# Cross attention on one Trainium2 core: the context's two halves made during self-attention and loaded from DRAM for each head

## The reference: what is computed

```
x = layernorm(x + self_attention(x))            # 16 heads of 128, causal
x = layernorm(x + cross_attention(x, ctx, ctx)) # below
x = layernorm(x + ffn(x))                       # ternary weights: signs of W_g, W_u, W_d

# cross_attention(q, k, v, gamma): 8 heads, cut along the rows
qh, kh, vh = (m.reshape(B, 8, 64, 512) for m in (q, k, v))   # k = v = context
qk  = einsum('bhdq,bhdl->bhql', qh, kh) / sqrt(64)
ret = einsum('bhql,bhdl->bhdq', softmax(qk), vh)
return gamma * ret.reshape(B, 512, 512)
```

## Time and profile before

| | us |
|---|---|
| median of three runs | 1504.17 (1502.49 to 1505.21) |
| the profiled execution | 1502.57 |
| its span, first to last instruction | 1500.8 |
| TensorE busy in the span | 1434.7 (96%) |
| VectorE | 1100.5 (73%) |
| ScalarE | 725.1 (48%) |
| GpSimd | 636.6 (42%) |

### The profile page before, as it was taken

The page is one execution under the profiler, slowest core; times in us unless marked ns, Lnnn a source line. Parts: engine busy times, 40 slices in busy tenths (PEclk is TensorE's granted clock), DMA queues, the critical chain, the costliest instruction groups (busy, mean ns, idle before and its releaser), DMA issues. The chain is left out here.

```text
span 1500.8 us, 24088 instructions
## 1 busy us (share of the span) xinstructions
PE 1434.7 (96%) x6988; PEld 1146.6 (76%) x7008; DVE 1100.5 (73%) x2368; ACT 725.1 (48%) x1549; POOL 636.6 (42%) x493
## 2 busy tenths in 40 slices
PE   7999999999999999999999999859999989999996
PEld 5788888888888888888888888737887765565564
DVE  4667677776777676777767776678999995796854
ACT  3444444545444444444353544438987863323332
POOL 1333424334243334242433433357887853343432
PEclk9999999999999999999999999979999999999998
DMA  6566666666656666666666664811224103000000
GB/s 175 155 166 169 167 169 163 167 161 166 161 164 160 161 161 171 167 165 164 162 167 158 168 166 133 210 50 54 60 60 151 36 1 112 1 29 28 0 29 28
DMA packets 193609, 185.09 MB, mean 123 GB/s; under 512 B 97057, under 2 KB 170785, under 8 KB 193313
## 3 DMA queue, kind: packets, MB, share of 16 engines
q1 hardware_dynamic: 192416, 184.09, 45.7%
q10 hardware_dynamic: 1152, 0.52, 0.2%
HBM read 113.25 MB, written 71.30 MB: 123 GB/s over the span
## 5 line engine op out<-in xcount | busy, mean ns | idle before, releaser
L583 ACT ACTIVATE probs<-probs,neg_max 128x128 f32<-128x128 f32 (+3 forms) x256 | 142.5, 557 | 357.8 <-DVE neg_max L707 350.2
L411 POOL TENSOR_TENSOR v_lo<-placed,v_hi 128x512 fp32r<-128x512 f32 x64 | 83.2, 1299 | 366.1 <-ACT v_hi L589 366.1
L413 POOL TENSOR_TENSOR pT_lo<-placed,pT_hi 128x1280 fp32r<-128x1280 f32 x64 | 189.2, 2956 | 0.0
L767 DVE SCALAR_TENSOR_TENSOR acc<-attn_bank,prob_recip,acc 128x512 f32<-128x512 f32 x256 | 174.8, 745 | 8.1 <-PE attn_bank L483 3.3
L1303 POOL TENSOR_TENSOR prod_lo<-prod,prod_hi 128x512 fp32r<-128x512 f32 x64 | 84.7, 1323 | 143.2 <-ACT prod_hi L1412 143.2
L707 DVE CUSTOM_DVE_ANT_0 probs<-attn_bank,mask 128x128 f32<-128x128 f32 (+3 forms) x256 | 117.2, 481 | 8.3
L682 DVE TENSOR_TENSOR qT_lo<-attn_bank,qT_hi 128x512 fp32r<-128x512 f32 x64 | 44.2, 691 | 105.2 <-ACT qT_hi L571 105.2
L950 POOL TENSOR_SCALAR xprobs<-xprobs,xprob_recip 128x512 f32<-128x512 f32 x128 | 99.9, 797 | 36.1 <-DVE xprob_recip L1130 36.0
L719 DVE STREAM_TRANSPOSE turned<-probs 128x256 f32<-128x256 f32 (+1 forms) x384 | 113.9, 362 | 0.0
L1362 PE MATMUL y_bank<-wdT_f32r,prod_hi 128*128 128x512 f32 x256 | 110.7, 432 | 2.3 <-POOL prod_lo L1303 1.8
L483 PE MATMUL attn_bank<-woT_hi,zT_hi 128*128 128x512 f32 x256 | 101.2, 395 | 8.9 <-DVE zT_lo L682 8.9
(11 more groups left out here) (145 smaller groups left out, 3887.5 us busy)
## 6 DMA issues: line engine op xcount, KB each, us to landing
turned_scratch<-turned SPq DMA_DIRECT2D x64, 896.0 KB, 3.9
placed<-turned_scratch SPq DMA_DIRECT2D x256, 224.0 KB, 4.3
rows_twice<-in_ctx_dram SPq DMA_DIRECT2D x64, 128.0 KB, 2.6
acc<-in_x_dram SPq DMA_DIRECT2D x16, 256.0 KB, 5.2
rows<-in_L_attn_W_V_dram SPq DMA_DIRECT2D x64, 64.0 KB, 2.3
rows<-in_L_attn_W_O_dram SPq DMA_DIRECT2D x64, 64.0 KB, 2.7
rows_twice<-in_L_ffn_W_g_dram SPq DMA_DIRECT2D x64, 64.0 KB, 3.1
rows_twice<-in_L_ffn_W_u_dram SPq DMA_DIRECT2D x64, 64.0 KB, 2.0
```

The source lines that it names most:

```text
L413: nc.gpsimd.tensor_tensor(pT[par][1][:], placed_probs, pT[par][0][:].bitcast(F32), ALU.subtract).then_inc(p_lo, 1)
L583: nc.scalar.activation(probs[:, cols], probs[:, cols], ACT.Exp, bias=low[:, par, t:t + 1], scale=-1.0, accum_out=total[:, par, t:t + 1]).t ...
L767: nc.vector.scalar_tensor_tensor(out=acc[:, b * NT + t, :], in0=s_bank[t][:], scalar=recip[:, b, t:t + 1], in1=acc[:, b * NT + t, :], op0= ...
```

## The change

The context's halves are made once for each of its 16 tiles of 128 rows, during self-attention, one tile at the end of each head's iteration, and are kept in DRAM as `context_halves`, where hi and lo of a row lie side by side (4 KB a row). For it:

- Slot 1 of the shared buffer (now `pair`) is lent to the context tile between two slices of `wu`. So `wu` is loaded at batch 1 of an iteration and not at batch 0, and the context tile at batch 3, when `wu` has been turned.
- GpSimd scales the tile by 1/8 in place, rounds it to hi and subtracts to lo (`split`, three operations of 128 x 512) behind the lo halves of batch 3. SP stores both, 512 KB, after the signs (`keep_halves`).
- In cross attention `load_halves` loads the 64 rows of a head twice, hi and lo together: two DMAs of 64 x 4 KB straight into the operand `cp`. It does so four heads ahead, once TensorE has scored the head that used the buffer; `split_context` is gone, and TensorE waits for the landing.
- The query halves are made as they were, with a scale of 1 in place of 1/8.

The diff, cut to its core:

```diff
+        self.kept = nc.dram_tensor("context_halves", (B, S, 2, D), F32).ap()
+        self.kept_tiles = self.kept.rearrange("b (t p) k d -> p (b t) k d", p=P)
...
-    def load_twice(self, sp, b, h):
-        for half in range(2):
-            sp.dma_start(self.twice[half * XD:(half + 1) * XD, h % 2, :],
-                         self.context[bass.ds(b, 1), h * XD:(h + 1) * XD, :].rearrange("o r d -> (o r) d")).then_inc(self.twice_loaded[h % 2], 16)
+    def load_split_tile(self, sp, n):
+        sp.dma_start(self.pair[:, 1, :], self.tiles[:, bass.ds(n, 1), :].rearrange("p o d -> p (o d)")).then_inc(self.split_loaded, 16)
+
+    def split(self, nc, pool, halves, k, n):
+
+        raw = self.pair[:, 1, :]
+        if not isinstance(n, int) or n > 0:
+            pool.wait_ge(self.halves_kept, n * 16)
+        wait_apart(pool, k, self.split_loaded, n * 16 + 16)
+        nc.gpsimd.tensor_scalar(raw, raw, XSCALE, 1.0, ALU.mult, ALU.mult).then_inc(self.scaled, 1)
+        wait_apart(pool, k, self.scaled, n + 1)
+        nc.gpsimd.tensor_scalar(halves[:, 0, :], raw, 1.0, 1.0, ALU.mult, ALU.mult).then_inc(self.split_hi, 1)
+        wait_apart(pool, k, self.split_hi, n + 1)
+        nc.gpsimd.tensor_tensor(halves[:, 1, :], raw, halves[:, 0, :].bitcast(F32), ALU.subtract).then_inc(self.split_done, 1)
+
+    def keep_halves(self, sp, halves, k, n):
+
+        wait_apart(sp, k, self.split_done, n + 2)
+        sp.dma_start(self.kept_tiles[:, bass.ds(n, 1), :, :].rearrange("p o k d -> p (o k) d"), halves[:].bitcast(F32)).then_inc(self.halves_kept, 16)
+
+    def load_halves(self, sp, cp, b, h):
+
+        for side in range(2):
+            sp.dma_start(cp[h % 2][side * XD:(side + 1) * XD, :, :],
+                         self.kept[bass.ds(b, 1), h * XD:(h + 1) * XD, :, :].rearrange("o r k d -> (o r) k d")).then_inc(self.halves_loaded[h % 2], 16)
...
                         load_gate_up(sp, "wg", h)
+                    if b == 1:
+                        wait_apart(sp, k, rows.split_done, h + 1)
                         load_gate_up(sp, "wu", h)
...
                         keep_signs(h, 0)
+                        wait_apart(sp, k, f_turn, h * 3 + 3)
+                        rows.load_split_tile(sp, h)
...
                         keep_signs(h, 2)
+                        rows.keep_halves(sp, halves, k, h)
...
                 loads(H - 1, 0, False)
                 exchange(FIRST + 2, 0)
+                loads(H - 1, 1, False)
                 loads(H - 1, 2, False)
                 keep_signs(H - 1, 0)
                 exchange(FIRST + 3, 1)
+                sp.wait_ge(f_turn, (H - 1) * 3 + 3)
+                rows.load_split_tile(sp, H - 1)
                 for m in (1, 2):
                     keep_signs(H - 1, m)
                 for t, name in enumerate(("wk", "wq", "wv", "wo")):
                     sp.wait_ge(w_turn[name], H)
                     rows.load_tile(sp, 0, t)
-                sp.wait_ge(f_turn, H * 3 + 1)
-                for h in range(2):
-                    rows.load_twice(sp, 0, h)
                 rows.load_gamma(sp)
+                rows.keep_halves(sp, halves, k, H - 1)
+                sp.wait_ge(rows.halves_kept, H * 16)
...
+                    if b == 3:
+                        rows.split(nc, pool, halves, k, h)
...
+                rows.split(nc, pool, halves, k, H - 1)
                 for b in range(2):
                     norm_gpsimd(nc, pool, norm, k.minus_half, b)
...
-        cp = [[sb(f"cp{i}_{p}", [P, D], F32R) for p in ("hi", "lo")] for i in range(2)]
+        cp = [sb(f"cp{i}", [P, 2, D], F32) for i in range(2)]
...
-                    nb, nh = ahead(b, h, 6)
-                    if exists(m + 6, ITEMS) and exists(m + 4, ITEMS):
-                        wait_count(sp, cp_ready, m + 5)
-                        source.load_twice(sp, nb, nh)
+                    nb, nh = ahead(b, h, 4)
+                    if exists(m + 4, ITEMS):
+                        if exists(m + 2, ITEMS):
+                            wait_apart(sp, k, scores_full, m * NT + 3 * NT)
+                        source.load_halves(sp, cp, nb, nh)
...
-                def split_context(b, h):
-
-                    par = h % 2
-                    wait_apart(pool, k, twice_loaded[par], b * (16 * XH) + 32 * (h // 2 + 1))
-                    nc.gpsimd.tensor_scalar(cp[par][0][:], twice[:, par, :], 1.0, 1.0, ALU.mult, ALU.mult).then_inc(cp_hi, 1)
-                    pool.wait_ge(cp_hi, b * XH + (h + 1))
-                    nc.gpsimd.tensor_tensor(cp[par][1][:], twice[:, par, :], cp[par][0][:].bitcast(F32),
-                                            ALU.subtract).then_inc(cp_ready, 1)
-
                 def step(b, h):
                     m = b * XH + h
-                    if exists(m + 4, ITEMS):
-                        if exists(m + 2, ITEMS):
-                            wait_apart(pool, k, scores_full, m * NT + 3 * NT)
-                        split_context(*ahead(b, h, 4))
...
-                        pe.wait_ge(cp_ready, nb * XH + (nh + 1))
+                        pe.wait_ge(source.halves_loaded[nh % 2], nb * (32 * PAIRS) + 32 * (nh // 2 + 1))
...
-                        last = nc.tensor.matmul(score_bank[t % 2][:], xs[nh % 2][:, t * P:(t + 1) * P], cp[nh % 2][p][:],
+                        last = nc.tensor.matmul(score_bank[t % 2][:], xs[nh % 2][:, t * P:(t + 1) * P], cp[nh % 2][:, p, :].bitcast(F32R),
...
-                                                 ACT.Copy, scale=XSCALE).then_inc(x_hi, 1)
+                                                 ACT.Copy, scale=1.0).then_inc(x_hi, 1)
```

More of the change, by code:

```diff
@@ L33 @@
 SCALE = 1.0 / math.sqrt(DH)
+XSCALE = 1.0 / math.sqrt(XD)
 MASKED = -1.0e10
@@ L91, in __init__ @@
         self.tiles = context.rearrange("b (t p) d -> p (b t) d", p=P)
+        self.kept = nc.dram_tensor("context_halves", (B, S, 2, D), F32).ap()
+        self.kept_tiles = self.kept.rearrange("b (t p) k d -> p (b t) k d", p=P)
         self.nat = [sb(f"rows{t}", [P, D]) for t in range(NT)]
-        self.twice = sb("rows_twice", [P, 2, D])
+        self.pair = sb("rows_pair", [P, 2, D])
         self.gamma = sb("gamma", [P, 1])
         self.nat_loaded = [sem(f"ctx_loaded{t}") for t in range(NT)]
-        self.twice_loaded = [sem(f"ctx_twice_loaded{i}") for i in range(2)]
+        self.split_loaded = sem("ctx_split_loaded")
+        self.scaled, self.split_hi, self.split_done = sem("ctx_scaled"), sem("ctx_hi"), sem("ctx_split")
+        self.halves_kept = sem("ctx_halves_kept")
+        self.halves_loaded = [sem(f"ctx_halves_loaded{i}") for i in range(2)]
         self.gamma_loaded = sem("gamma_loaded")
@@ L234, in attention @@
         f_turned = sb("f_turned", [P, D])
-        raw_ffn = rows.twice
+        raw_ffn = rows.pair
+        halves = sb("ctx_halves", [P, 2, D], F32R)
         sign_gu = [sb(f"sign_{n}", [P, NC, P], BF16) for n in ("g", "u")]
@@ L1514, in __init__ @@
         self.wait_value = {}
-        self.unused = sb("unused", [P, 8])
+        self.unused = sb("unused", [P, 16])
         self.started = 0
```

10 lines of the change are left out of this document (4 added, 6 removed).

## The result

| | median us (runs) | profiled execution, span us | GpSimd busy us | bytes moved MB |
|---|---|---|---|---|
| before | 1504.17 (5) | 1502.57, 1500.8 | 636.6 | 185.09 |
| after | 1512.22 (5) | 1510.67, 1508.8 | 615.0 | 206.07 |

The ratio is 1.0054, with an interval of 1.0041 to 1.0067: slower by 8.0 us at the medians. The forecast was 1508.0 with a range of 1504.2 to 1512.0; the median lies 0.2 us outside it.

What follows compares the result with a forecast made beforehand. TensorE was taken as the bound, busy 96% of the span, with VectorE taking over beside the last norms. Terms −1.3 + 2.7 + 0.3 + 1.9 + 0.2 = +3.8 us gave 1508.0 us, range 1504.2 to 1512.0.

Steps and rivals of the forecast that it cites:

- 1 relief: Cross attention: with GpSimd's split gone, VectorE's norm operations get shorter; −1.3 us, bounds 0 and 3.3.
- 2 split: End of self-attention: the last split's three GpSimd operations delay the norm powers; +2.7 us, bounds 2.5 and 3.2.
- 3 SP's row: End of self-attention: the later wu load pushes SP's scratch write and copies back; +0.3 us, bounds 0 and 1.9.
- 4 first load: Start of cross attention: head 0's load, behind two row tiles, delays the first score; +1.9 us, bounds 0.8 and 3.8.
- 5 signs: Late cross attention: head 21's half-pair queues behind the sign transfers; +0.2 us, bounds 0 and 3.
- The other 15 splits: End of each self-attention iteration: about 5 us of cover before SP's next necessary issue, so 0.
- The upper bound of 3.8 us: First load of cross attention: its cost if it lands in 5.2 us, like 256 KB x tiles in a full queue.
- the loads to one half of the partitions are slow: Cross attention: first load 3.0, head 21's wait 1.5 to 2.5, clock one more; +7.7 us, 1511.9 us, chance 0.17.
- head 21 not or barely waiting: Sign expected in the profile after: TensorE's score of head 21 waits little or not at all for its load.
- its bound of 3 us: Load of the signs: the cost if head 21's half-pair needs its own 2.8 us and more after the signs land.

Runs made afterwards that it cites:

- the second profile: The changed kernel, unaltered, profiled once more to see what repeats: 1509.18 us in one run.
- the second experiment: Changed kernel with the loads of the halves of heads 0 and 1 issued first in cross attention, ahead of the row tiles: 1510.02 us, ratio 1.0035.

## Why the prediction was wrong

| term | forecast | measured | by |
|---|---|---|---|
| 1 relief | −1.3 | −1.42 | marks 1133 to 1229, six kernels without the wait |
| 2 split | +2.7 | +2.78 | both pairs of profiles; undone, the wait is 7.32 |
| 3 SP's row | +0.3 | +0.3 and 0.0 | third to last to last pT_lo: 24.72 and 23.31 us, before 24.40 and 23.27 |
| 4 first load | +1.9 | +3.7 and +2.8 | both pairs |
| 5 signs | +0.2 | +1.5 and +1.8 | marks, with the relief taken out |

**Terms 1 and 2** were right, by their own reasoning. The split's price is its three operations, because nothing stood between pT_lo and the power. The relief came where VectorE's norm stood beside GpSimd, and exactly two of the eight operations became free, as counted; the third, counted by a part, did not, and 0.4 us of the relief came from elsewhere. **Term 3** can't be told from nothing: the two profiles of one kernel differ by 1.1 to 1.4 us there. The other 15 splits cost little or nothing: from the second pT_lo to the third to last it took 885.5 and 885.9 us before, and 885.9 in both profiles after.

**Term 4 is the step that failed.** I let the first load land in 2.8 us, the time of a 256 KB tile that goes to 128 partitions with an almost empty queue. The issue went out where I had it: the second of head 0's loads 2.24 us behind the first transposes, forecast 2.3. But it landed 5.13 us later, and 4.22 in the second profile. The experiments part this in two:

- The pair's own landing. With nothing in front of it it took 4.06 us, 1.3 more than I had, and with half of the bytes 2.94. In the steady part the two forms stand side by side in the profile after: 3.9 us to 64 partitions and 2.8 to 128 (the former come in pairs, though, and share the queue with each other).
- The two rows in front, which cost it another 1.1 us in the first profile and 0.2 in the second.

I wrote that a MB goes through the queue here; with head 1's loads, which SP issues right behind head 0's, it is 1.5 MB. That slip cost little, as the second experiment shows.

Why the pair is slow shows in the DMA columns. From 1003 to 1005 us only the loads of the halves were under way; the rows had landed 2.6 and 2.8 us after their issue. The DMA engines were busy throughout, at 229 GB/s, and at 217 in the second profile (1001 to 1003 us, share 0.97). With the signs, which go to 128 partitions, they reached 442 at a like share, in the same kernel.

```profile
1003.00:1005.00 2.00, 0.00 (x0) 0.00 (x0) 0.00 (x0) 0.00 (x0) 0.00 (x0) 0.50 1.01 229
```

```profile
1146.00:1148.00 2.00, 2.00 (x12) 1.63 (x11) 1.88 (x4) 1.77 (x4) 0.68 (x1) 1.00 1.04 442
```

The last two columns are the DMA share and GB/s. The upper bound of 3.8 us was right; choosing 1.9 was not, and I had named the nearest row by its size instead of by its form. At the start the form is only one of two causes, and undoing it alone brought nothing (wait 6.41 us); the order alone brought 1.8 to 2.7 us, and the form on top of it 0.9 (first score 4.68 and then 3.79 us behind the transposes). Why one transfer of 512 KB took 5.91 us behind the rows and 3.79 in front of them stays open.

This is what the Trainium skill, page "SBUF — State Buffer", section "Door 1: The DMA port swizzle (why [64,N] ≈ [32,N])", says: a transfer to 64 partitions has at most about 218 GB/s, and two of them do not add up. The trace agrees, with 229 and 217.

**Term 5 failed by the same mistake.** Head 21's pair stood behind 4 MB of signs, and I gave it the stretch's 418 GB/s and the signs their old landing of 13.1 us. The second transfer of the signs landed in 15.5 us and the pair's second load 1.68 us behind it (forecast 1.25); TensorE waited for it for 1.69 us. With one transfer to 128 partitions per head the signs took 14.1 us and head 21's load landed 1.26 us behind them, and the wait was gone; so it was with the signs in pieces. The second sign transfer took 15.5 to 16.2 us in all six profiles in which it shared the queue with full pairs, and 14.1 to 14.4 in the four with one load per head: the pairs slowed the signs too, head 20's goes out just in front of them. The prediction's sign "head 21 not or barely waiting" did not come, but its bound of 3 us held. The size is uncertain: six profiles have the changed kernel's code at this place, and there the cost runs from 1.0 to 3.8 us.

**The rival that came true** is the second, "the loads to one half of the partitions are slow", with term 4 at 3.0, head 21 at 1.5 to 2.5 and +7.7 in all. It had a chance of 0.17. What spoke against it in the text, 418 GB/s for the whole queue, was measured on transfers to 128 partitions, so it said nothing of this form. That its 1511.9 us stands 0.3 from the median is in part luck, as the sum shows.

**Sum.** 2.8 + 3.2 + 1.65 − 1.4 + 0.15 (means of the two pairs) = +6.4 us, where the forecast had +3.8; the medians say +8.0. A ratio of 1.0043, which is what +6.4 us would give, lies inside the measured interval and makes 1510.6 us, below the range's end: the terms explain 2.6 of the 4.2 us that were missed, and without the rest the time would have stood inside. Part of it goes with the clock. Over 139 runs of 11 kernels, each against its own kernel's mean, a mean granted clock higher by 0.001 goes with a time shorter by 0.48 us (uncertain by 0.05), and it accounts for 47% of the scatter. The five runs of the changed kernel had a mean clock of 0.9804, 62 runs of before 0.9829: 1.2 us. Whether the change makes the clock fall more often, or five runs were unlucky, stays open: the one later run, at 0.983, lay 6.3 us above its chip's median of before, which is what the sum says. I had put one us of clock into the rival; its mean size was right, but the stage from the first score to 1133 us moved by +1.7 in one pair and by −1.0 in the other.

## What to carry to other kernels

- Price a transfer by a row of its own form, not of its size alone: the same 256 KB took 2.8 us to 128 partitions and 3.9 us to 64, in pairs, and doubling the bytes in DRAM to load 512 KB in one transfer to 128 partitions took 3.2.
- What is loaded first in a block must be issued first; two lines in another order were worth 1.8 to 2.7 us at the first score here, more than the 1.42 us of relief that the change could bring.
- Work that moves off a chain has to go somewhere: look for a stretch in which its engine is idle and the other engine does not read and write SBUF alone; beside the wrong neighbour, or with its input still under way, half of the gain comes back.

## What the runs showed of the hardware

- GpSimd's split stretches VectorE's tensor_scalar from SBUF to SBUF to 1.8 times its length (four in 3.49 us against 1.91), but not scalar_tensor_tensor with an operand in PSUM (2.73 us for four, beside the split and alone).
- In the two profiles in which TensorE waited for 2.6 and 2.7 us at head 21, the 20 us that hold the wait had a mean clock of 0.91; in the four with a wait of 1.1 to 2.1 us there was no such fall. The stretch between the marks was 3.77 us longer with the wait of 2.70, of which the wait itself makes 2.2: the 0.49 us at the head's fourth tile are gone in return.
- Spells at 1.2 GHz after 990 us differ from run to run of one kernel: executions of one version spread from 1498.84 to 1505.94 us, at mean clocks of 0.987 and 0.979. The last stage, from 1229 us before to the end, took 269.1 and 271.8 us in the two profiles of the changed kernel. A profile pair alone can therefore mislead by 2 to 3 us in either direction in a stage that the change does not touch.
